# Two chained attention layers on one core: values as scaled float16 pairs, the crossbar writing the value product's operand, value units summed in PSUM

## The reference

```python
# layer 0: d = 64
theta, phi = conv1x1(x, W_theta, b_theta), conv1x1(x, W_phi, b_phi)
f = softmax(theta^T phi / sqrt(64))            # 1024 x 1024
x1 = x + conv1x1(x f^T, W_fuse, b_fuse)
# layer 1: c = 128
h = group_norm(x1, 32 groups) * gn_w + gn_b
q, k, v = conv1x1(h, ...), conv1x1(h, ...), conv1x1(h, ...)
out = x1 + conv1x1(v softmax(q^T k / sqrt(128))^T, p_w, p_b)
```

## Time and profile before

| what | value |
|---|---|
| median of three runs | 2164.61 us |
| the profiled execution | 2154.83 us |
| its span, first to last instruction | 2152.9 us |
| mean granted TensorE clock | 0.957 of 2.4 GHz |
| busy share of PE, DVE, ACT, POOL | 85%, 78%, 73%, 72% |
| DMA share of 16 engines | 67.6% |

### The profile page before, as it was taken

One profiled execution on the slowest core, in us unless ns is written; L12 is line 12 of the kernel. 1 busy time (PEld: TensorE's weight loads), 2 busy tenths in 40 slices (PEclk: granted clock), 3 DMA queues, 4 the chain that ended last, 5 costly groups with the idle time before them and its releaser, 6 DMA issues. The chain is left out here.

```text
span 2152.9 us, 33388 instructions
## 1 busy us (share of the span) xinstructions
PE 1823.9 (85%) x8388; PEld 1451.8 (67%) x8388; DVE 1671.4 (78%) x1706; ACT 1567.4 (73%) x2281; POOL 1540.3 (72%) x1605
## 2 busy tenths in 40 slices
PE   5888889888888888898888898888988888888887
PEld 4666767666667666676666676666766666766765
DVE  5778778878787777787787877877877878777774
ACT  5778768777777777687777777776877777777764
POOL 4687677776687776777766877767777668777665
PEclk9899999999999999999999999999999999999999
DMA  5577676666677676777666876767767668757664
GB/s 103 113 142 146 117 148 140 139 140 126 118 156 141 126 139 122 144 142 139 138 127 119 154 141 124 142 126 139 142 134 143 123 121 156 141 125 139 125 127 90
DMA packets 860086, 286.32 MB, mean 133 GB/s; under 512 B 822305, under 2 KB 823201, under 8 KB 860065
## 3 DMA queue, kind: packets, MB, share of 16 engines
q1 hardware_dynamic: 860064, 286.08, 67.6%
HBM read 50.86 MB, written 17.04 MB: 32 GB/s over the span
## 5 line engine op out<-in xcount | busy, mean ns | idle before, releaser
L756 POOL TENSOR_SCALAR et<-pair_t 128x2048 fp32r<-128x2048 f16 x384 | 731.7, 1908 | 86.0 <-DMA pair_t<-pair 83.3
L630 DVE TENSOR_REDUCE neg_max<-s_ps 128x1 f32<-128x1024 f32 x512 | 623.0, 1217 | 207.1 <-PE s_ps L371 195.5
L371 PE MATMUL o_ps<-et,v_hi 128*128 128x512 f32 x2048 | 764.9, 415 | 21.0 <-DVE y_sb L679 17.6
L647 DVE SCALAR_TENSOR_TENSOR pair<-s_ps,pair 128x1024 f16<-128x1024 f32 x384 | 467.4, 1217 | 40.5 <-ACT pair L587 40.0
L371 PEld LDWEIGHTS o_ps<-et,v_hi 128*128 128x128 f32 x2048 | 395.8, 193 | 110.3 <-DVE y_sb L679 20.3
L564 ACT ACTIVATE s_ps<-s_ps,neg_max 128x1024 f32<-128x1024 f32 x384 | 417.0, 1086 | 20.8 <-DVE neg_max L630 13.8
L371 PE MATMUL s_ps<-phi,theta 128*128 128x512 f32 x1024 | 308.2, 427 | 138.8 <-DVE pair L647 138.0
L587 ACT ACTIVATE pair<-s_ps 128x1024 f16<-128x1024 f32 x384 | 392.9, 1023 | 21.6
L371 PE MATMUL o_ps<-et,v_lo 128*128 128x512 f32 x1024 | 408.6, 399 | 0.0
L371 PEld LDWEIGHTS s_ps<-phi,theta 128*128 128x128 f32 x1024 | 205.2, 205 | 195.8 <-issue 141.7
L820 POOL TENSOR_TENSOR stage<-stage 128x256 f32<-128x256 f32 x256 | 200.6, 784 | 181.0 <-ACT stage L520 157.5
(11 more groups left out here) (89 smaller groups left out, 2533.5 us busy)
## 6 DMA issues: line engine op xcount, KB each, us to landing
rden_row<-rden_dram SPq DMA_DIRECT2D x128, 256.0 KB, 4.3
xs<-in_x SPq DMA_DIRECT2D x32, 512.0 KB, 5.1
phi<-phi SPq DMA_DIRECT2D x64, 256.0 KB, 4.1
out_y<-y_sb SPq DMA_DIRECT2D x64, 256.0 KB, 2.4
pair_t<-pair SPq DMA_TRANSPOSE x384, 4.4
rden_dram<-rden SPq DMA_DIRECT2D x128, 2.0 KB, 1.4
w_f<-in_w_fuse_t SPq DMA_DIRECT2D x1, 64.0 KB, 2.5
ident_sb<-in_ident SPq DMA_DIRECT2D x1, 64.0 KB, 2.3
```

The lines of the kernel that those rows point to most:

```text
L371: mm = pe.matmul(out, lhs_t, rhs, start=start and n == 0, stop=stop and n == len(terms) - 1)
L630: nc.vector.tensor_reduce(neg_max[:, t % 4:t % 4 + 1], s_ps[:, part(t), :], AX.X, ALU.max, negate=True).then_inc(s_max, 1)
L647: nc.vector.scalar_tensor_tensor(out=pair[:, r, 1, :], in0=s_ps[:, part(t), :], scalar=E_SCALE, in1=pair[:, r, 0, :], op0=ALU.mult, op1=AL ...
L756: return nc.gpsimd.tensor_scalar(*args)
```

## The change

- The values become float16 pairs (`v_hi`, `v_lo`), and so does `et`. The crossbar transposes straight into `et`, which now holds four groups; `pair_t` and the casts are gone. The value product's moving operand is four runs of 128 columns.
- So that float16 holds them, values are scaled by 16384 over a bound. For layer 0 the bound is made per image: `x_maxima` (VectorE), a row of it (GpSimd), the product `mx` with |W_fuse| (TensorE), and `value_scale` (VectorE: maximum, clamp, reciprocal). For layer 1 it is made once. The reciprocal of the denominators takes the scale back (`den_scaled`).
- A value unit makes four blocks, and its three terms add up in PSUM; four value units are left of eight.
- ScalarE copies every q, k, v and w unit to `stage` in two places, and GpSimd splits it (`split_units`). VectorE's rest of q and k is gone.
- Layer 0's residual sum, `xr`, `x_hi` and `x1_res` move to GpSimd; the bias of the fusion is added in `xr`.
- `PART`, `UNITS`, the lags and the slots change; in two slots VectorE takes the rest ahead of the maximum.

The rest of the diff is names of semaphores, the set-up of the weights' bounds before the loop, and the waits that follow from the new order.

```diff
-CAST_LAG = 4
-PV_LAG = 7
-OUT_LAG = 11
+PV_LAG = 6
+OUT_LAG = 10
...
-PART = (0, 1, 2, 0, 1, 2, 0, 1, 2, 0, 1, 2, 0, 1, 0, 2)
+PART = (0, 1, 0, 2, 1, 0, 2, 1, 0, 2, 0, 1, 2, 0, 1, 2)
+SHORT = (0, 8)
...
-UNITS = {0: "gn1", 1: "gn2", 2: "v2", 3: "v3", 4: "k0", 5: "k1", 6: "q0", 7: "w0", 8: "q1", 9: "tp0", 10: "w1",
-         11: "tp1", 12: "w2", 13: "w3", 14: "v0", 15: "v1"}
-STAGES = 4
-STAGE = {name: n % STAGES for n, name in enumerate(UNITS[s] for s in range(SLOTS) if UNITS[s][0] in "vw")}
-X_SLOT = 6
-X_LO_SLOTS = (7, 9)
-XR_SLOT = 1
-XS_SLOT = 2
+V_TOP = 16384.0
+BOUND_MIN = 1e-20
+
+NORM_MAX = 64.0
+
+UNITS = {0: "gn1", 1: "gn2", 4: "k0", 5: "k1", 6: "q0", 7: "q1", 8: "w0", 9: "mx", 10: "tp0", 11: "w1", 12: "tp1",
+         14: "v0", 15: "v1"}
+STAGE = {"k0": 0, "k1": 1, "q0": 0, "q1": 1, "w0": 0, "w1": 1, "v0": 0, "v1": 1}
+STAGES = 2
+XR_SLOT = 0
+XS_SLOT = 1
+X_SLOT = 4
+X_LO_SLOTS = (6, 8)
 H_SLOT = 2
 H_LO_SLOTS = (3, 4)
-RES_SLOTS = (5, 9)
-PHI_SLOTS = {10: "tp0", 12: "tp1"}
+RES_SLOTS = (3, 7)
+PHI_SLOTS = {11: "tp0", 13: "tp1"}
...
+        v_hi = [sb(f"v_hi{n}", [P, KB, C], F16) for n in range(2)]
+        v_lo = [sb(f"v_lo{n}", [P, KB, C], F16) for n in range(2)]
+        stage = sb("stage", [P, STAGES, HALF])
...
+        et = sb("et", [P, SLOTS // GROUP, GROUP, 2 * KB, P], F16)
...
-                sp.wait_ge(s_et, before(crossed_at, it, t - GROUP + 1))
+                sp.wait_ge(s_pv, et_free(it, t))
                 sp.sem_inc(s_carrier)
-                sp.dma_start_transpose(pair_t[:, r, :, :],
+                sp.dma_start_transpose(et[:, t // GROUP % 4, r, :, :],
...
-                    pe.wait_ge(s_et, before(crossed_at, it, first + GROUP))
+                    for r in range(PAIRS):
+                        pe.wait_ge(s_pair_t[r], 16 * before(same_pair(r), it, first + GROUP))
                     pe.wait_ge(s_tlo, before(turned_at, it, first + GROUP))
-                    if first == 0:
-                        pe.wait_ge(s_split, before(values_at, it, 4))
-                    if first == PHASE:
-                        pe.wait_ge(s_split, before(values_at, it, 14))
+                    if first % SLOTS == 0:
+                        pe.wait_ge(s_split, before(staged_at, it, first))
+                    if first % SLOTS == PHASE:
+                        pe.wait_ge(s_split, before(staged_at, it, first + 4))
                     pe.wait_ge(s_taken, before(group_at, it, first))
-                g = first // GROUP % 2
+                g = first // GROUP % 4
                 for kb in (2 * quarter, 2 * quarter + 1):
-                    mm = product(o_ps[:, :], [(v_hi[layer][:, kb, :], et[g][:, 0, kb, :]),
-                                              (v_lo[layer][:, kb, :], et[g][:, 0, kb, :]),
-                                              (v_hi[layer][:, kb, :], et[g][:, 1, kb, :])],
+                    mm = product(o_ps[:, :], [(v_hi[layer][:, kb, :], et[:, g, :, kb, :]),
+                                              (v_lo[layer][:, kb, :], et[:, g, :, kb, :]),
+                                              (v_hi[layer][:, kb, :], et[:, g, :, KB + kb, :])],
                                  start=kb == 0, stop=kb == KB - 1)
...
-                pe.wait_ge(s_evac, before(unit_at, it, s))
-                pe.wait_ge(s_direct, before(direct_at, it, s))
+                pe.wait_ge(s_evac, before(taken_at, it, s))
+                pe.wait_ge(s_tp, before(tp_at, it, s))
+                pe.wait_ge(s_bound[0], before(mx_at, it, s))
...
+                elif name == "mx":
+                    pe.wait_ge(s_w_abs, 1)
+                    pe.wait_ge(s_x_row, before(mx_at, it, s) + 1)
+                    mm = pe.matmul(m_ps[:, 0:C], x_max_row[:, :], w_f_abs[:, :], start=True, stop=True)
...
-                        for b in range(2):
-                            px = slice((2 * part + b) * P, (2 * part + b + 1) * P)
-                            pe.matmul(m_ps[:, 2 * b * C:2 * (b + 1) * C], hi[:, px],
-                                      w[:, :, :].rearrange("p a c -> p (a c)"), start=True, stop=False)
-                            mm = pe.matmul(m_ps[:, 2 * b * C:(2 * b + 1) * C], lo[:, px], w[:, 0, :],
-                                           start=False, stop=True)
+                        for b in range(GROUP):
+                            px = slice((GROUP * half + b) * P, (GROUP * half + b + 1) * P)
+                            mm = product(m_ps[:, b * C:(b + 1) * C], [(hi[:, px], w[:, 0, :]), (lo[:, px], w[:, 0, :]),
+                                                                      (hi[:, px], w[:, 1, :])])
...
-                elif name[0] in "vw":
-                    act.wait_ge(s_split, or_none(before(values_at, it, s) + 1 - STAGES))
-                    nc.scalar.activation(stage[:, STAGE[name], :, :, :],
-                                         m_ps[:, :].rearrange("p (b t c) -> p b t c", b=2, t=2),
-                                         ACT.Copy).then_inc(s_evac, 1)
+                    return
+
+                act.wait_ge(s_split, or_none(before(staged_at, it, s) + 1 - STAGES))
+                to = stage[:, STAGE[name], :]
+                if name[0] in "vw":
+                    layer = int(name[0] == "w")
+                    act.wait_ge(s_scale[layer], 1 if layer else before(mx_at, it, s))
+                    nc.scalar.activation(to, m_ps[:, :], ACT.Identity,
+                                         scale=v_scale[layer][:, 0:1]).then_inc(s_evac, 1)
                 else:
-                    act.wait_ge(s_scores, before(tile_at, it, 0))
-                    hi, bias = (q_hi, vec_ready[:, 1:2]) if name[0] == "q" else (k_hi, vec[:, B_K:B_K + 1])
-                    nc.scalar.activation(hi[:, cols], m_ps[:, :], ACT.Identity, bias=bias).then_inc(s_evac, 1)
...
+            def value_scale(layer, src, n):
+
+                nc.vector.tensor_reduce(bound[layer][:, :], src, AX.X, ALU.max).then_inc(s_bound[layer], 1)
+                dve.wait_ge(s_bound[layer], n)
+                nc.vector.tensor_scalar(clamped[layer][:, :], bound[layer][:, :], BOUND_MIN, 1 / V_TOP, ALU.max,
+                                        ALU.mult).then_inc(s_clamped[layer], 1)
+                dve.wait_ge(s_clamped[layer], n)
+                dve.sem_inc(s_carrier)
+                nc.vector.reciprocal(v_scale[layer][:, :], clamped[layer][:, :]).then_inc(s_scale[layer], 1)
...
+                nc.vector.tensor_scalar(den_scaled[:, :], den[:, g, :], v_scale[layer][:, 0:1], E_SCALE, ALU.mult,
+                                        ALU.mult).then_inc(s_den, 1)
+                dve.wait_ge(s_den, n + 1)
 
                 dve.wait_ge(s_rden_dram[g], 16 * before(same_group(first), it, first))
-                nc.vector.reciprocal(rden[:, g, :], den[:, g, :]).then_inc(s_rden, 1)
...
-                nc.vector.scalar_tensor_tensor(out=x1[:, cols], in0=x1[:, cols], scalar=vec[:, B_FUSE:B_FUSE + 1],
-                                               in1=xr[:, cols], op0=ALU.add, op1=ALU.add).then_inc(s_x1, 1)
...
+            def x_maxima(it, s):
+                if not here(x_at, it, s):
+                    return
+                n = before(x_at, it, s)
+                dve.wait_ge(s_xs, 16 * (n + 1))
+
+                dve.wait_ge(s_x_row, n)
+                nc.vector.tensor_reduce(x_max[:, :], xs[:, :], AX.X, ALU.max,
+                                        apply_absolute_value=True).then_inc(s_x_max, 1)
...
+                if here(mx_at, it, s):
+                    n = before(mx_at, it, s) + 1
+                    dve.wait_ge(s_unit, before(unit_at, it, s) + 1)
+                    value_scale(0, m_ps[:, 0:C], n)
...
+                    if s - 2 in SHORT:
+                        take_lo(it, s)
+                        maxima(it, s)
+                    else:
+                        maxima(it, s)
+                        take_lo(it, s)
                     normalised(it, s)
-                    unit_lo(it, s)
+                    take_unit(it, s)
                     reciprocals(it, s)
-
-                    outputs(it, s - 1, 0)
+                    x_maxima(it, s)
                     statistics(it, s - 2, 0)
-                    outputs(it, s, 1)
-                    statistics(it, s, 1)
+                    statistics(it, s - 1, 1)
...
-            def casts(it, s):
-                t = s - CAST_LAG
-                if not here(crossed_at, it, t):
-                    return
-                r, g = t % GROUP, t // GROUP % 2
-                cols = slice(t % GROUP * P, (t % GROUP + 1) * P)
-                pool.wait_ge(s_pair_t[r], 16 * before(same_pair(t), it, t) + 16)
-                if t % GROUP == 0:
-
-                    pool.wait_ge(s_pv, or_none(before(group_at, it, t) - 1))
-                scaled(et[g][:, :, :, cols].rearrange("k a b q -> k (a b) q"), pair_t[:, r, :, :], 1.0, 1.0,
-                       ALU.mult, ALU.mult).then_inc(s_et, 1)
...
+            def split_units(it, s):
```

(49 more changed lines are left out.)

227 lines of the change are left out of this document (109 added, 118 removed).

## The result

The changed kernel takes **2085.35 us** (median of four runs, 2083.53 to 2085.83) against 2162.97 us for the kernel before in the same comparison. The ratio is 0.9641, with a 95% interval of 0.9625 to 0.9658. The forecast was 1986. So the direction was right and the time lies in the range, but less than half of the forecast gain came: 78 us instead of 179.

A forecast was written before the change was run, and what follows sets the result against it. No engine was saturated; TensorE, busy 85%, lost time to stalls. Work 54.0 + stalls 5.2 + handovers 0.3 gave 59.5 us per image against 65.4: -183 us, +4 at the start, 1976 profiled, 1986 us median; range 1895 to 2110.

The forecast's parts named there:

- The boundary stall and its slow clock: TensorE before tile 0's scores of a new image: 4.6 us stall plus 2.7 us of half-clock work, expected to go.
- TensorE's work: TensorE's products and units per image: 53.2 us before, 54.0 after (-1.3 float16, +1.8 value units, +0.3 bound product).
- a rival with 0.17: Value product: float16 runs at full rate, term -3.2 instead of -1.3, 57.6 us per image, 1927 us; chance 0.17.
- The value block: Value units on TensorE: three weight loads per block, 0.34 us against 0.225, +1.8 us per image.
- some 50 us: Value product: if float16 behaves like bfloat16 at 215.7 ns, term -2.9 us and the total some 50 us lower.
- The waits: TensorE's remaining stalls per image, at slots 2, 6, 8, 10 and 11: 5.2 us in sum.
- the same walk: Walk through one image from the start of tile 0's scores, listing TensorE's stalls up to slot 11: 5.2 us.
- The form of the sum: Period per image: TensorE's work 54.0 plus stalls 5.2 plus 0.3 for handovers gives 59.5 us.
- GpSimd's order: GpSimd's queue before q0 and q1 delays scores(8): 2.5 us more per image, 62.0 us, 2064 us; chance 0.18.
- the port lock: Five small VectorE multiplications stand behind GpSimd operations, up to 1.28 us each: +6.4, 65.9 us, 2184 us; chance 0.08.
- DMA: Transposes write the operand directly, landing in 4.4 us; they and the earlier image load fit, cost 0.
- The ends: Program start, outside the image periods: a chain for the weights' bounds adds about +4 us.

The follow-up runs named there:

- the best version: Changed kernel with slot 14 normalising before its maximum and GpSimd splitting the queries ahead of its other work: 2034.9 us, ratio 0.9419 to the kernel before.
- half maxima: Changed kernel with slot 14 normalising first and queries split first, plus each tile's maximum over 512 of 1024 columns and a smaller exponential scale: ratio 0.892.

## Why the prediction fell short, point by point

**The boundary stall and its slow clock, -7.3 us per image: right in kind, half in size.** The 4.58 us stall is gone, and the pair order alone brings 111 us, 3.6 per image. What the step missed is that new waits come up behind it even then: of 4.6 us for the stall and 2.7 for the clock half arrived.

**TensorE's work, 54.0 us: nearly right, 52.6 measured.** The products came at the full rate, 0.216 us, so the term was -2.4 (from a mean of 0.240) and not -1.3; that case I had called a rival with 0.17. The Trainium skill's 215.7 ns for bfloat16 ("TensorE: Matmul & The Clock Gate", Part 1) agrees with the 0.216 us of float16 in this trace. The value block takes 0.336 us, the forecast 0.34. But the time that either was to bring or cost did not come: 9 to 15 us where the rate says 75, 12 where the sums say 55. The "some 50 us" beside the page's figure took the same false step, that TensorE's work counts in full.

**The waits, 5.2 us: this is the step that failed.** Measured on the same walk (forecast, then trace, us per image):

| wait of TensorE | forecast | after |
|---|---|---|
| slot 2, bank of tile 0 | 0.8 | 1.19 |
| slot 2, normalisation | 1.2 | 1.08 |
| slot 4, transposes behind the exponential | 0 | 0.53 |
| slot 6, normalisation | 0.2 | 0.78 |
| slot 8, query split | 0.9 | 1.15 |
| slot 10, bank of tile 8 | 0.2 | 0.65 |
| slot 10, `tp0` behind the bound | 1.05 | 0.99 |
| slot 11, `w1` behind `phi` | 0.85 | 0.68 |
| slot 14, normalisation | 0, not walked | 1.98 |
| slow clock behind it, every second image | 0 | 0.9 |
| sum | 5.2 | 9.9 |

The places that I walked came out within 0.6 us each. The walk stopped at slot 11, where two float32r rests, two denominators' steps, a maximum, a rest and the normalisation pile up on VectorE within 7 us, and there lay the largest wait. I also wrote that no wait resembled the one before the slow clock. One of 1.81 us was enough to be followed by it [timeline above].

**The form of the sum failed too.** It adds TensorE's work to a fixed list of waits. The runs show that the list isn't fixed: it closes up behind TensorE. Work taken from it makes the waits longer, and work given to it makes them shorter. At one clock a microsecond of TensorE's work was worth 0.14 to 0.28 (float16 0.34 of 2.4, PSUM sums 0.50 of 1.8, extra products 0.91 and 0.67 of 3.6), and the removed wait of 1.98 us in slot 14 0.18. The removed waits of slots 2 and 6 cost more than they gave, and only the 1.15 us of slot 8 came back in full (62.12 to 60.90). On one and the same version 114 us more on TensorE cost 11, or 21 at one clock, while a shorter link of the hand-over, with only 273 - 209 = 64 us less on VectorE in all, brought 79. And the sum had no term for how often the slow clock strikes, which moved the four runs of one kernel by up to 33 us.

**GpSimd's order.** The rival gave it 2.5 us more; the wait is 1.15, close to the 0.9 of the forecast. Taking it away gave 30 us, the one wait that paid in full at one clock.

**VectorE and the port lock.** The rival with 0.08 (a slower kernel) did not come. The scalings have a median of 0.22 us, a mean of 0.27 and at most 0.42 in the kernel after. In the best version, whose GpSimd order is another, one of the four per image does stand behind GpSimd (below): 29 of its 128 take over 0.6 us, and the mean is 0.42. No run shows what this costs there.

**DMA: right.** The transposes land in 4.4 us as before, and nearly no value product waits for them.

**The ends: +4 forecast, +16 measured.** The first score product starts at 32.23 us and not at 20.19. In front of it lie the weights' bound (TensorE waits 4.20 us for `w_pv_abs`) and the maximum of x (a wait of 10.3 us for its row, where the kernel before waited 8.7 for `x_lo`). Sum: (62.65 - 59.5) x 31 = 98 us from the period and 12 from the ends, 110 against the profiled execution of 2085.3 where the forecast had 1976.

**What stays open.** That the hand-over from the scores to the rest sets the period is shown in its first link. The exponential, the copy and the rest were not shortened. The runs with extra TensorE work on the kernel after spread over 33 us, and the clock goes with them (0.987 to 0.973); what makes the slow clock catch more images in one run than in another is open. Of the 34 us that the change costs beside the pair order, 13 lie outside the 31 periods (141 against 128 us) and 22 in them (62.65 against 61.94). Which part of the change makes them is open; the two waits that were mended (slots 14 and 8) make up more than that.

## What to carry over

When an engine is busy 85% and its remaining waits are small and many, its work and its waits don't add: each wait ends at a time that a chain through other engines sets, so price an edit by what it does to that chain. Compare images at the same clock before you say that two edits don't add: a time in which the slow clock strikes more or less often hides up to the whole of a small gain. Walk all slots, the crowded ones of the neighbouring engine first, and test with one run that adds known work to the supposed bound: 114 us that cost 11, or 21 at one clock, say more than any table of waits. And test the smallest part alone; here the order of the bank pairs gave more than the whole.

## What the runs showed of the hardware

- **A float16 weight load takes half of a float32r one.** The groups of the kernel after, 99 against 193 ns for the same 128x128 block:

```profile
L392 PEld LDWEIGHTS o_ps<-et,v_hi 128*128 128x128 f16 x2048 | 202.6, 99 | 363.3 <-issue 143.1 <-DVE y_sb L719 39.2
L392 PEld LDWEIGHTS s_ps<-phi,theta 128*128 128x128 f32 x1024 | 193.7, 193 | 112.9 <-DVE pair L682 56.0 <-DVE et L676 2.6 <-DVE bound L637 0.7
```

- **A small VectorE operation can stand a whole GpSimd operation long.** In the timelines of the kernel with half maxima a scaling of four columns takes 1.00 us and ends with GpSimd's rest (1026.26 + 1.28); alone it takes 0.22:

```profile
1026.57 1.00 DVE L694 TENSOR_SCALAR den_scaled<-den,v_scale 128x4 f32<-128x4 f32 x1
1057.46 0.22 DVE L694 TENSOR_SCALAR den_scaled<-den,v_scale 128x4 f32<-128x4 f32 x1
...
1026.26 1.28 POOL L806 TENSOR_TENSOR x_lo<-xs,x_hi 128x512 fp32r<-128x512 f32 x1
```

The same at the start of the kernel after: the 128x128 rest of `w_pv` takes 1.27 us beside GpSimd's `v_lo`, that of `w_q` 0.29 while GpSimd is idle. This fits the exclusive lock of the Trainium skill ("SBUF — State Buffer", SBUF: two separate sides), and it is the rival's mechanism.
- **The slow clock came after waits of 1.8 us, not only after 4.6, and after smaller ones.** In the best version it starts within 0.3 us of a value product that had waited 0.9 us, 2 us behind a wait of 1.0, and does so in about every second image. And it comes and goes with the order: 0.957 before, 0.983 after, 0.994 when the best version's TensorE had more to do. Part of what a removed wait brings is this, and added work can bring it as well.
